# Table-product picks of layer 1 all built on ScalarE instead of on ScalarE and VectorE in turn

## What is computed

```python
h = jnp.maximum(_layernorm(x, axis=-1), 0.0)
x = x + segment_sum(h[src] * edge_weight[:, None], dst)           # layer 0
h = jnp.maximum(_layernorm(x, axis=-1), 0.0)
# layer 1, for every edge: an MLP makes 4 matrices of 8x8 ...
hid = jax.nn.relu(edge_feat @ W1 + b1)
w = (hid @ W2 + b2).reshape(e, 4, MUL, MUL)
w_000, w_011, w_101, w_110 = (w[:, 0], w[:, 1], w[:, 2], w[:, 3])
s_e = s[src]; v_e = v[src]                                        # rows of h
m0 = ALPHA * (einsum('ei,eio->eo', s_e * sh0[:, None], w_000) + C110 * einsum('eim,em,eio->eo', v_e, sh1, w_110))
m1 = ALPHA * (einsum('ei,em,eio->eom', s_e, sh1, w_011) + einsum('eim,eio->eom', v_e * sh0[:, None, None], w_101))
out0 = segment_sum(m0, dst) + SI_SCALE * (s @ si_w0)
out1 = segment_sum(m1, dst) + SI_SCALE * einsum('nim,io->nom', v, si_w1)
x = x + concatenate([out0, out1])
```

## Time and profile before

| | us |
|---|---|
| median of 3 runs | 6243.72 |
| lowest and highest | 6241.42, 6246.52 |
| the profiled execution | 6246.71 |
| its span, first to last instruction | 6244.9 |

### The profile page before, as it was taken

One profiled execution on the slowest core, in us unless ns is written; L12 is line 12 of the kernel. 1 busy time (PEld: TensorE's weight loads), 2 busy tenths in 40 slices (PEclk: granted clock), 3 DMA queues, 4 the chain that ended last, 5 costly groups with the idle time before them and its releaser, 6 DMA issues.

```text
span 6244.9 us, 161388 instructions
## 1 busy us (share of the span) xinstructions
PE 6088.4 (97%) x44043; PEld 4996.6 (80%) x44043; DVE 5563.4 (89%) x13227; ACT 3634.2 (58%) x14178; POOL 4668.2 (75%) x4915
## 2 busy tenths in 40 slices
PE   6999999999999999996999999999999999999998
PEld 5888888888888888885777777777777777777776
DVE  7888888778777787775999999999999999999999
ACT  3222222222222222224888888888888888888886
POOL 6777777777777777776777777777777777777776
PEclk9999999999999999997999999999999999999998
DMA  4111111111111111112111111112121111111121
GB/s 113 34 32 34 34 33 33 34 34 32 34 32 34 34 32 34 34 33 42 41 40 42 41 40 40 41 42 42 40 43 40 41 42 42 40 43 40 40 43 37
DMA packets 290300, 247.19 MB, mean 40 GB/s; under 512 B 105284, under 2 KB 286740, under 8 KB 289800
## 3 DMA queue, kind: packets, MB, share of 16 engines
q0 software_dynamic: 156256, 80.32, 9.4%
q1 hardware_dynamic: 133212, 163.33, 9.3%
q10 hardware_dynamic: 802, 3.22, 0.2%
HBM read 241.24 MB, written 5.25 MB: 39 GB/s over the span
## 4 chain that ended last, share of the span: by engine, by line
POOL 28%; PE 15%; issue 10%; POOLq 0%; DVE 0%; ACT 0%; DMA 0%; DVEq 0%; ACTq 0%
POOL z L486 28%; PE hp_ps L924 7%; PE w_ps L853 3%; PE sc_ps L877 1%; PE w_ps L842 1%; PE w_ps L850 1%; PE sc_ps L880 1%; PE sc_ps L885 0%; PE w_ps L815 0%; POOLq L483 0%; DMA z<-h_table,idx 0%; POOLq L287 0%; POOLq L484 0%; POOLq L482 0%; DVE x_sb L1187 0%
## 5 line engine op out<-in xcount | busy, mean ns | idle before, releaser
L486 POOL DMA_INDIRECT z<-h_table,idx x4883 | 4635.9, 949 | 1498.2 <-issue 1471.6
L770 PE MATMUL w_ps<-parts,pick 128*128 128x448 f32 x12110 | 2551.4, 369 | 69.3 <-DVE pick L1078 56.7
L770 PEld LDWEIGHTS w_ps<-parts,pick 128*128 128x128 f32 x12110 | 2257.5, 188 | 279.6 <-issue 70.3
L613 ACT ACTIVATE z<-z,squares 128x32 f32<-128x32 f32 x3132 | 726.8, 309 | 2045.0 <-DMA z<-h_table,idx 1933.5
L924 PE MATMUL hp_ps<-parts,pick 128*128 128x448 f32 x7224 | 1601.4, 372 | 0.0
L924 PEld LDWEIGHTS hp_ps<-parts,pick 128*128 128x128 f32 x7224 | 1316.1, 188 | 262.4 <-issue 163.0
L1078 DVE TENSOR_TENSOR pick<-sc_ps,feat 128x896 fp32r<-128x896 f32 x865 | 906.1, 1080 | 4.3 <-DMA feat<-key_table 4.1
L853 PE MATMUL w_ps<-w_sb,squares 64*128 64x256 f32 x6264 | 842.9, 378 | 0.0
L853 PEld LDWEIGHTS w_ps<-w_sb,squares 64*128 64x128 f32 x6264 | 722.8, 187 | 73.0 <-issue 0.3
L1244 DVE TENSOR_TENSOR prod<-w_ps,squares 128x384 f32<-128x384 f32 (+1 forms) x1044 | 778.8, 746 | 0.9 <-ACT squares L674 0.9
L711 ACT ACTIVATE squares<-iota_sb,rel_sb 128x32 f32<-128x32 f32 x3132 | 713.7, 307 | 0.0
(11 more groups left out here) (95 smaller groups left out, 5328.1 us busy)
## 6 DMA issues: line engine op xcount, KB each, us to landing
z<-h_table,idx POOLq DMA_INDIRECT x4883, 2.4
feat<-key_table SPq DMA_DIRECT2D x345, 192.0 KB
squares<-in_ft_sh SPq DMA_DIRECT2D x261, 216.0 KB
feat<-key_table SPq DMA_DIRECT2D x173, 128.0 KB
h_table<-big SPq DMA_DIRECT2D x10, 280.0 KB
rel_sb<-in_dst_t SPq DMA_DIRECT2D x1, 1566.0 KB, 8.6
idx_all<-in_src_t SPq DMA_DIRECT2D x1, 1530.0 KB, 10.1
squares<-in_ew_t SPq DMA_DIRECT2D x1, 1530.0 KB, 14.1
```

The lines of the kernel that those rows point to most:

```text
L486: pool.indirect_dma_start(z[:, r, u, :], None, rows, bass.IndirectOffsetOnAxis(ap=idx[:, r, u:u + 1], axis=0)).then_inc(z_in[r], 16)
L613: last = nc.scalar.activation(z[:, r, u, :], z[:, r, u, :], ACT.Copy, scale=ew_all[:, bass.ds(n * G + u, 1)])
L770: mm = pe.matmul(fold_ps[:, pick_banks[k], 0:NC * D], pick[:, k, blk, :], parts[:, t, :, blk, :], start=(blk == 0 and t == 0), stop=(blk = ...
```

## The change

ACT makes the pick of every supertile that has one, in the way it made the odd ones. `make_pick1`, the choice `pick_by_act` and the count `pick_turn` go, and DVE makes no picks in layer 1. The two semaphores `pick1_by_dve` and `pick1_by_act` become one, `pick1_ready`, which PE and SP wait on; SP waits once for a batch of keys instead of twice. The three buffers, the batches of keys and the order of everything else stay.

```diff
-    def pick_by_act(r):
-        return r % 2 == 1
-
-    def pick_turn(b, r):
-        return (b - 1) * (R1 // 2) + r // 2 + 1
...
                     if s is None or s >= R1:
-                        for t in (at + 1, at + 2):
-                            sp.wait_ge(pick1_by_act if pick_by_act(t) else pick1_by_dve, pick_turn(b, t))
-                            sp.nop(nofuse=True)
+                        sp.wait_ge(pick1_ready, nth(b, at + 2) + 1)
+                        sp.nop(nofuse=True)
...
                 last.then_inc(rows_off, 1)
-                act.wait_ge(rows_off, pick_turn(b, t))
-                nc.scalar.activation(off, off.bitcast(F32), ACT.Relu, scale=-1.0, bias=one_sb[:]).then_inc(pick1_by_act, 1)
+                act.wait_ge(rows_off, nth(b, t) + 1)
+                nc.scalar.activation(off, off.bitcast(F32), ACT.Relu, scale=-1.0, bias=one_sb[:]).then_inc(pick1_ready, 1)
...
-                if pick_by_act(t) and (s is None or R1 <= s + 4 < S):
+                if s is None or R1 <= s + 4 < S:
                     rows_away(bt, t, s)
...
-                    pe.wait_ge(pick1_by_act if pick_by_act(t) else pick1_by_dve, pick_turn(bt, t))
+                    pe.wait_ge(pick1_ready, i + 1)
...
-            def make_pick1(b, r, s):
-
-                bt, t = before(b, r, R1, -4)
-                dve.wait_ge(keys1_in[t // BATCH], bt * 16)
-                if s is None or s + 4 >= R1 + RING1:
-                    dve.wait_ge(picked1, nth(bt, t) - RING1 + 1)
-                nc.vector.tensor_tensor(pick[:, t % RING1], rows_ps.unsqueeze(2).to_broadcast([P, GB, P]),
-                                        key1[:, t].unsqueeze(1).to_broadcast([P, GB, P]), ALU.is_equal
-                                        ).then_inc(pick1_by_dve, 1)
...
-                    if not pick_by_act((r + 4) % R1) and (s is None or R1 <= s + 4 < S):
-                        make_pick1(b, r, s)
                     if s is None or 2 <= s <= S + 1:
                         reduce_sums(q).then_inc(sum1_reduced, 1)
```

More of the change, by code:

```diff
@@ L268, in gnn_two_layers @@
         table1_in, split1_act, split1_dve = sem("table1_in"), sem("split1_act"), sem("split1_dve")
-        pick1_by_dve, pick1_by_act, rows_off, picked1, group1_step, selected1 = (
-            sem(n) for n in ("pick1_by_dve", "pick1_by_act", "rows_off", "picked1", "group1_step", "selected1"))
+        pick1_ready, rows_off, picked1, group1_step, selected1 = (
+            sem(n) for n in ("pick1_ready", "rows_off", "picked1", "group1_step", "selected1"))
         idx1_ready, z1_in = (sems(n, R1) for n in ("idx1_ready", "z1_in"))
```

## The result

The changed kernel takes 6586.19 us, the median of 4 runs (6585.53 to 6586.31), the kernel before 6245.12 us beside it (6241.42 to 6278.6, 4 runs). The ratio is 1.054, with a 95% interval from 1.051 to 1.057: 5.4% slower. The forecast was 6604.5 us with a range of 6570 to 6650. The profiled execution of the changed kernel took 6586.31 us.

What follows compares the result with a forecast made beforehand. PE, DVE and POOL were taken to run level near 6.28 us a turn, with ACT next at 6.99. 6246.7 + 364 (514 turns) - 3 at the ends = 6607.7, less 3.0 for the median: 6604.5 us, range 6570 to 6650.

Steps and rivals of the forecast that it cites:

- The pacer before: Layer 1 before the change: PE 6.23, DVE 6.32, POOL 6.24 us a turn, mean 6.28; relieving one alone could give 0.05.
- The pick on ACT, 3.13 us: In ACT's turn, a pick was to push the next relu back 3.13 us: seven overlapping distances and one relu.
- The estimate from the Trainium skill: Alternative cost of ACT's eight pick activations: 2991 ns, making the sum 36 us less, 6568 us.
- The mean turn of 6.99: ACT's turn in layer 1 after the change, averaged over a round of six: 41.95 / 6 = 6.99 us.
- the turn of 7.23: ACT's longest turn with a pick in a round of six; 0.12 us taken off for loop jump or perhaps row wait.
- the turns without a pick: ACT's three light turns, 3.88, 3.81 and 3.88 us without waits, were to become 7.01, 6.94 and 7.01.
- the ends of the stage: Start and end of layer 1: 1 us lost on a pick, 3 to 4 us of ACT's row wait gained, together -3.
- What lies beside it: Nothing was to add to ACT's 6.99 us turn: PE's 6.23, POOL's 6.24 and DVE's 5.65 can run beside it.
- An ACT turn under 6.9 us: Sign in the profile after that would show the forecast wrong; starts 6.9 to 7.1 us apart were expected.
- more than ACT's own work: Rival: engines waiting on one another in layer 1 add 0.1 to 0.5 us a turn, 6655 to 6860 us; chance 0.09.
- DVE was the pacer and ACT's pick would hide: Rival: ACT keeps up and PE's 6.23 us sets the turn, -27 us, 6217 us; chance of faster 0.015.
- The rule by which DVE, as the engine with the highest occupancy, was the one to relieve: Trainium skill's rule, DVE first with 99%: by it alone the turn goes to 5.65 us, the time to about 5920.

## Why the prediction was right

*The pacer before.* The prediction had PE, DVE and POOL within 0.1 us of one another, and a gain on DVE capped at 0.05 us a turn. The runs confirm the cap and more: without even picks nothing was gained. Of the three it is POOL that set 6.28, by gathers held up beside DVE, with PE's 6.23 or 6.27 next to it. The prediction had read POOL's 6.24 and not the long gathers in it; this changed nothing in the sum, which started from the measured 6.28. (The 2963.9 and 6193.0 us that this rests on are starts of the activation, and the prediction calls the first its end; the distance between them is the same.)

*The pick on ACT, 3.13 us.* It held. In the changed kernel the relu (L659) starts 3.22 us after the copy of the indices (L550), where 3.23 were read with a pick and 0.10 without: a pick costs 3.12 us. The estimate from the Trainium skill (ScalarE: Activation LUTs, What ACT_TABLE_LOAD costs) was 2.99, and the sum by it, 6568 us, misses by as much on the other side. What it lacked can be read from the rows: the relu of the pick does not overlap the distances by 0.09 but starts 0.03 us after their end, and it takes 1.042 us instead of 1.026; 2.991 + 0.093 + 0.032 + 0.016 = 3.13.

*The mean turn of 6.99.* It measured 6.955, and this is the term that was mis-sized: 514 x 0.035 = 18 us. More than half of it is the turn of 7.23, of which 0.12 us was taken for the loop's jump. There is no such cost, since all turns of the changed kernel take 6.98 or 6.895 us. The 0.24 us too many stand between the relu and the scalars, which start 0.70 us apart there (4531.47 and 4532.17) and 0.46 in the other turns with a pick; in the trace the last of the gathered rows landed at 4531.92, so it was a wait for rows, which the prediction named as the other possibility. The rest comes from the turns without a pick. They were counted at 7.01, 6.94 and 7.01 with one added and came at 6.98 or 6.895. They held an L671 that had waited, and behind such a one the next activation starts 0.20 us later (4512.46 - 4512.26), behind one that has not waited 0.17 (4506.78 - 4506.61): the waits were taken off, and this 0.03 that comes with them was not.

*Errors that cancelled.* For the profiled execution the forecast was 6607.7 us and 6586.3 was measured, 21.4 less: 18 by the mean turn and 3 at the ends of the stage, where 6 us were gained and 3 forecast. The median was then set 3.0 us under the profiled execution, as it lay before the change; the runs of the changed kernel lie within 1 us of one another. That the mean turn alone seems to explain the 18.3 us between 6604.5 and 6586.2 is luck.

*What lies beside it.* Nothing, as forecast: DVE's comparison put back costs at most 5 us, one semaphore or two nothing, and 0.29 us of added work on ACT costs 0.29 us a turn. PE waited for ACT's relu in each turn for about 0.6 us (0.7 forecast), at full clock.

*Signs.* L676 3612 and L679 516 times, ACT at nine tenths and DVE at 84%: as forecast. An ACT turn under 6.9 us was to be a sign of being wrong; two turns in six took 6.895, so this sign stood too close to the forecast to tell anything. DVE was to wait for ACT; it waited for PE's weights (264.8 us, above), which come behind ACT's relu. POOL was to wait for `msg1_ready`; it waited for ACT's copy of the indices, which ACT makes late in its turn (218.6 us, above). POOL was turns ahead of ACT by then, and ACT never waited for rows, so it cost nothing.

*The rivals.* That more than ACT's own work would show did not happen: no run needed it. That DVE was the pacer and ACT's pick would hide is refuted twice, by the picks left out and by the pick without its relu, which needed ACT's turn under 6.25 to come back to the old time. The rule by which DVE, as the engine with the highest occupancy, was the one to relieve would have given 5920 us; with DVE alone relieved, the kernel took 6275, against 6255 for the kernel before beside it.

## What to carry to other kernels

When engines run level, count the turn of the engine that takes the work, not the one that gives it: ACT's idle time was 15%, and that was 438 us where the move needed 748. Read the new turn off the timeline as the longest present turn repeated, less its waits, and compare it with the pace of all others before moving anything. Before relieving the engine that looks full, find out by leaving its work out whether it sets the pace; here an engine at 99% did not, and one that looked three quarters busy did.

## What the runs showed that was not expected

A gather issued by POOL takes 0.94 us, and longer, up to 1.4 us, when it begins from 0.3 us before to 0.1 us after the start of DVE's product vsh; it then ends 1.11 to 1.20 us after that product began, whenever it began itself. Since POOL's turn is a hair longer than PE's, this made a kernel with less work slower (6275 us, and 6234 with a gather taken away). It may also be why the kernel before spread from 6237 to 6291 us between runs, while the changed one stayed within 1 us; that was not tried.

PE's fourteen matmuls of a pick take 3.10 us in some turns and 3.13 in others, in long stretches of one execution, at a granted clock of 1.00, so PE's shortest turn is 6.23 or 6.27 us. Runs of one kernel fall into two groups about as far apart as this makes over 514 turns.

A wait of ACT on its own result costs 32, 97 or 116 ns of idle time, by the order and place of the two waits of that instruction.
